# Down projection of a mixture of experts with the weights stationary and 512 tokens moving

## The reference

```
x = x + tanh(g_xattn) * attention(layernorm(x), ctx, ...)
x = x + tanh(g_ffn) * ffn(layernorm(x))
# ffn:
g = einsum('btd,edf->ebtf', x, gate_w)
u = einsum('btd,edf->ebtf', x, up_w)
h = silu(g) * u
expert_out = einsum('ebtf,efd->ebtd', h, down_w)
out = einsum('ebtd,bte->btd', expert_out, combine)
```

## Time and profile before

| | |
|---|---|
| median of 3 runs | 266.81 us (266.63 to 267.21) |
| profiled execution, its own time | 266.45 us |
| its span, first to last instruction | 264.6 us |
| TensorE busy | 235.4 us, 89% |
| weight loads busy | 167.3 us, 63% |
| VectorE busy | 181.1 us, 68% |
| ScalarE, GpSimd busy | 91.5 and 93.4 us |
| mean granted TensorE clock | 0.968 of full speed |

### The profile page before, as it was taken

How to read it: one execution, slowest core, us unless ns; L and a number is a source line. 1 busy time by engine, 2 the same in 40 slices (tenths; PEclk the granted TensorE clock), 3 DMA queues, 4 the chain that set the end, 5 groups by cost and what they waited for, 6 DMA issues and landing times.

```text
span 264.6 us, 3797 instructions
## 1 busy us (share of the span) xinstructions
PE 235.4 (89%) x1275; PEld 167.3 (63%) x1275; DVE 181.1 (68%) x388; ACT 91.5 (35%) x171; POOL 93.4 (35%) x105
## 2 busy tenths in 40 slices
PE   0895695999989999999869899799999999999992
PEld 0762351455645555555525688688888888888882
DVE  2659979467696767776874475968857675776564
ACT  1564224355555665563556421010101010101100
POOL 5364590020374053621430010408934653462000
PEclk9999577799999999999999999999999999999999
DMA  7461660001900002020020000002312211000004
GB/s 207 75 216 45 154 144 20 2 0 24 201 17 1 2 1 59 2 59 0 1 63 0 0 4 0 0 2 61 81 41 59 59 23 39 0 0 2 0 0 160
DMA packets 22259, 12.09 MB, mean 46 GB/s; under 512 B 14784, under 2 KB 21472, under 8 KB 22240
## 3 DMA queue, kind: packets, MB, share of 16 engines
q1 hardware_dynamic: 21936, 11.63, 17.8%
q10 hardware_dynamic: 304, 0.22, 0.5%
HBM read 7.91 MB, written 1.05 MB: 34 GB/s over the span
## 4 chain that ended last, share of the span: by engine, by line
PE 73%; DVE 14%; issue 3%; SPq 3%; DMA 3%; ACT 2%; DVEq 0%
PE bank L955 66%; DVE mneg L811 3%; PE bank L1016 2%; DMA mqk_u<-in_mask_SxS_bc 2%; PE bank L1012 2%; DVE xn L671 1%; SPq L365 1%; DVE x_sb L948 1%; DVE w L853 1%; PE bank L1029 1%; DMA q<-q 1%; PE bank L1021 1%; DVE pT L883 1%; DVE q L889 1%; DVE q L680 1%
## 5 line engine op out<-in xcount | busy, mean ns | idle before, releaser
L955 PE MATMUL bank<-xT,cT 128*128 128x512 f32 x288 | 70.2, 392 | 0.0
L955 PEld LDWEIGHTS bank<-xT,cT 128*128 128x128 f32 x288 | 53.7, 188 | 12.0 <-issue 0.8
L811 DVE TENSOR_REDUCE mneg<-bank 128x4 f32<-128x512 f32 x64 | 43.3, 685 | 20.8 <-PE bank L955 20.4
L636 ACT ACTIVATE pT<-bank 128x512 f32<-128x512 f32 x64 | 38.5, 601 | 31.1 <-PE bank L955 30.1
L623 ACT ACTIVATE pT<-bank 128x512 f32<-128x512 f32 x24 | 14.4, 598 | 84.2 <-PE bank L955 84.2
L955 PE MATMUL bank<-q,kz 112*128 112x512 f32 x64 | 39.0, 611 | 0.0
L955 PEld LDWEIGHTS bank<-w_d,q 128*128 128x128 f32 x288 | 37.1, 188 | 2.8 <-issue 1.3
L955 PE MATMUL bank<-w_d,q 128*128 128x256 f32 x288 | 38.0, 281 | 0.8 <-DVE q L889 0.8
L955 PE MATMUL bank<-kz,q 96*128 96x512 f32 x64 | 28.7, 455 | 6.1 <-DVE mneg L811 5.9
L883 DVE TENSOR_TENSOR pT<-pT,bank 128x512 f32<-128x512 f32 x24 | 16.5, 686 | 16.6 <-PE bank L955 16.3
L874 DVE TENSOR_TENSOR pT<-pT,bank 128x512 f32<-128x512 f32 x24 | 16.4, 682 | 16.7 <-PE bank L955 16.7
(11 more groups left out here) (127 smaller groups left out, 302.8 us busy)
## 6 DMA issues: line engine op xcount, KB each, us to landing
padf<-in_L_ffn_down_w SPq DMA_DIRECT2D x12, 128.0 KB, 2.2
c_sb<-in_ctx SPq DMA_DIRECT2D x2, 512.0 KB, 6.4
q<-cT SPq DMA_DIRECT2D x8, 128.0 KB, 2.4
out<-x_sb SPq DMA_DIRECT2D x4, 256.0 KB, 2.4
q<-xn SPq DMA_DIRECT2D x8, 96.0 KB, 2.2
c_sb<-in_L_ffn_gate_w SPq DMA_DIRECT2D x8, 96.0 KB, 2.1
c_sb<-in_L_ffn_up_w SPq DMA_DIRECT2D x8, 96.0 KB, 2.1
x_sb<-in_x SPq DMA_DIRECT2D x2, 256.0 KB, 3.8
```

Of the source, the lines that this page charges most:

```text
L636: nc.scalar.activation(pT[:, i // 4, i % 4, :], bank[2 + s % 2][:], ACT.Exp, scale=SCALE).then_inc(p_done, 1)
L811: nc.vector.tensor_reduce(mneg[:, r, 4 * hf:4 * hf + 4], bank[n % 2][:].rearrange("p (g k) -> p g k", g=4), X, ALU.max, negate=True).then_ ...
L955: return nc.tensor.matmul(dst, a, b, start=start, stop=stop, skip_group_check=True)
```

## The change

The down projection takes w_d as the stationary operand (two chunks k of 128 output channels) and 512 tokens of h as the moving one: 6 matmuls of 512 columns in place of 12 of 256. The result lies in banks 2 to 5 with output channels on partitions, one bank for each half and chunk. It must be transposed back: the bank is copied to `y_sb` (which lies in `xb_sb`, no longer used by then), by ScalarE for three of the four banks and by VectorE for the last; TensorE transposes 128x128 pieces with the identity into `y_bank` (banks 2 and 3 for half 0, banks 6 and 7 for half 1); VectorE adds them to x_sb, 512 columns at a time.

The order of units changes for tiles 9 to 11: all three for half 0 and then all three for half 1. `END0`, the last unit of half 0, is 20. Half 0 goes back within the loop, behind down(21) on TensorE and behind weigh(22) on VectorE; half 1 at the very end.

```diff
-        ORDER = [(t, h) for h in range(NQ) for t in range(WR)] + [(t, h) for t in range(WR, FT) for h in range(NQ)]
+        ORDER = ([(t, h) for h in range(NQ) for t in range(WR)]
+                 + [(t, h) for t in range(WR, FT - WR) for h in range(NQ)]
+                 + [(t, h) for h in range(NQ) for t in range(FT - WR, FT)])
+        END0 = max(n for n, (_, h) in enumerate(ORDER) if h == 0)
...
+        def y_bank(h, pair):
+
+            return bank[(2, 3, 6, 7)[2 * h + pair]]
...
+            def output_chunk(h, k):
+
+                sc.wait_ge(y_done, 2 * ((END0 if h == 0 else len(ORDER) - 1)) + k + 1)
+                nc.scalar.copy(y_sb[:, h, k], bank[2 + DC * h + k][:]).then_inc(ya_ok, 1)
+
             for n in range(len(UP_SLOT), len(ORDER)):
                 silu(n)
+                if n == min(END0 + UL, len(ORDER) - 1):
+                    output_chunk(0, 0)
+                    output_chunk(0, 1)
+            output_chunk(1, 0)
...
+            def add_outputs(h):
+
+                for p in range(2):
+                    ve.wait_ge(yt_done, 2 * h + p + 1)
+                    t = h * TPH + 2 * p
+                    nc.vector.tensor_tensor(x_sb[:, t:t + 2], y_bank(h, p)[:].rearrange("p (t d) -> p t d", t=2),
+                                            x_sb[:, t:t + 2], ALU.add).then_inc(fin_ok, 1)
...
                 if n + UL < len(ORDER):
                     gated(n + UL)
-
-            for y in range(NB // 2):
-                ve.wait_ge(y_done, 2 * (len(ORDER) - NQ + y // 2) + y % 2 + 1)
-                for t in (2 * y, 2 * y + 1):
-                    ins = nc.vector.tensor_tensor(x_sb[:, t], bank[2 + y][:, t % 2 * D:(t % 2 + 1) * D], x_sb[:, t], ALU.add)
-                ins.then_inc(fin_ok, 1)
+                if n == END0 + 1:
+                    add_outputs(0)
+            ve.wait_ge(y_done, 2 * len(ORDER))
+            nc.vector.tensor_copy(y_sb[:, 1, 1], bank[2 + DC + 1][:]).then_inc(yd_ok, 1)
+            add_outputs(1)
...
-                for u in range(TPH):
-                    ins = three(bank[2 + (h * TPH + u) // 2][:, u % 2 * D:(u % 2 + 1) * D],
-                                [lambda c, i=i: (hh, hl)[i][:, n % 2, toks(u)] for i in range(2)],
-                                [lambda c, i=i: w_d[i][:, s] for i in range(2)], 1, first=(t == 0 and u % 2 == 0))
-                    if u % 2:
-                        ins.then_inc(y_done, 1)
+                for k in range(DC):
+                    three(bank[2 + DC * h + k][:], [lambda c, i=i: w_d[i][:, s, k * P:(k + 1) * P] for i in range(2)],
+                          [lambda c, i=i: (hh, hl)[i][:, n % 2] for i in range(2)], 1, first=(t == 0)).then_inc(y_done, 1)
+
+            def outputs_back(h):
+
+                if h:
+                    pe.wait_ge(*emptied(JOBS[-1]))
+                    pe.wait_ge(*emptied(JOBS[-2]))
+                for k in range(DC):
+                    if k == 0:
+                        pe.wait_ge(ya_ok, 2 if h == 0 else 3)
+                    elif h:
+                        pe.wait_ge(yd_ok, 1)
+                    for u in range(TPH):
+                        ins = nc.tensor.transpose(y_bank(h, u // 2)[:, u % 2 * D + k * P:u % 2 * D + (k + 1) * P],
+                                                  y_sb[:, h, k, toks(u)], ident)
+                        if k and u % 2:
+                            ins.then_inc(yt_done, 1)
...
                 down(n)
+                if n == END0 + 1:
+                    outputs_back(0)
+            outputs_back(1)
```

More of the change, by code:

```diff
@@ L175, in build @@
         pick_n = sb("pick_n", [2 * E, FT * P], U8)
+        y_sb = xb_sb[:].rearrange("p b d -> p (b d)").rearrange("p (h c n) -> p h c n", h=NQ, c=DC)
         pick_r = w_t[:, 0:FT * P]
@@ L244, in build @@
         fin_ok = sem("fin_ok")
+        ya_ok = sem("ya_ok")
+        yd_ok = sem("yd_ok")
+        yt_done = sem("yt_done")
         PHASE_A = [("wkv",), ("c", 0, 0), ("c", 0, 1), ("wq",), ("x", 0, 0), ("x", 0, 1), ("bias",), ("kv", 0),
```

## The result

The changed kernel takes 269.14 us (median of 6 runs, 268.33 to 269.90) against 267.01 us before: ratio 1.008, 95% interval 1.0054 to 1.0105. It is slower by 2.1 us. A second comparison on another occasion gave 1.007 (1.0046 to 1.0095).

A forecast was written before the change was run, and what follows sets the result against it. It took TensorE as the bound (89% busy, full in the feed-forward stage), with another order of work at the end. Terms -0.8 + 0.2 + 2.36 = +1.76 us gave 268.5 us, range 267.5 to 269.6.

The forecast's parts named there:

- The new down: Down projection on TensorE: 6 matmuls of 512 columns take 1.37 us in place of 1.41, 0.04 us less a step.
- the sum over the steps: Down projection gain over the 20 downs ahead of down(20): -0.8 us, bounds -0.4 to -1.2.
- The wait at up(20): TensorE waits ahead of up(20) for GpSimd's split of tile 11's gate and up weights: 0.19, say +0.2 us.
- The tail: From down(20) to the end of the span: +14.50 us against +12.14 before, a loss of 2.36 us.
- The late down(23): Down(23) on TensorE starts at +7.37 us after down(20) where it started at +5.93: +1.44 us.
- the way behind it: After down(23): copy, transposes and adds no longer overlap a projection, making the last add another 1.89 us later.
- the 1.44 us: Delay of down(23), laid to four adds of half 0 queued on VectorE ahead of weigh(23).
- The last transfer: Last output transfer at the end: lands after 2.3 us in place of 3.3, -1.0 us; bounds 2.2 and 3.3.
- Rival 1: Last output transfer lands no sooner, still 3.3 us: +1.0 us, 269.5 us in all; chance 0.12.
- Rival 3: Weight loads limit TensorE, so halving down's loads saves 14 us over 20 steps, some 255 us; chance 0.05.

The follow-up runs named there:

- The first two experiments: Changed kernel with half 0's two adds behind weigh(23): 268.33 us, 1.0038; then also CB(23) issued ahead of half 0's transposes: 268.36 us, 1.0023.
- the form alone: Kernel before with only the new down projection, old order and end, no transposing back (output holds transposed blocks): 266.82 us, ratio 0.9979.
- the order alone: Kernel before with only the new order of units, and the waits of its last adds set accordingly: 267.66 us, ratio 1.0008.
- the wide adds with clears: Kernel before with four last adds of 512 columns for eight of 256, plus four tiny VectorE clears as filling: 267.31 us, ratio 1.0005.
- the changed kernel with clears: Changed kernel plus four tiny clears in VectorE's idle time in the middle of the feed-forward stage: 268.65 us, ratio 1.005.
- the wide adds alone: Kernel before with its eight last adds of 256 columns made four of 512: 266.48 us, ratio 0.9968.
- both half-mixed kernels: Changed kernel, CB(23) first, half 0's adds behind weigh(23), half 1 in old down: 266.07 us, 0.9954; with half 1's last adds 512 wide: 266.31 us, 0.9966.
- the kernel with CB(23) first: Changed kernel with half 0's adds behind weigh(23) and CB(23) issued ahead of half 0's transposes on TensorE: 268.36 us, ratio 1.0023.

## Why the prediction was right, and where it was not

**The new down was priced nearly right, the sum over the steps was too large.** For the down 1.37 us were forecast and the rows show 1.40; a regular step is 4.367 us (forecast 4.35). That is 0.026 us won a step and not 0.04. Besides, I multiplied by 20 downs, and only 17 of them lie between the first full up and down(20). The other three lie ahead of that up. Behind the last of them TensorE idles for VectorE (1.62 us in before, 1.63 in after), and a gain of hundredths ahead of that wait cannot be told from the scatter of the start. 17 x 0.026 is 0.44 us where I had 0.8. Of these 0.44 the waits for GpSimd take 0.18 at up(20) and 0.08 at up(8), and another 0.03 is lost between the first up and down(3), which leaves the 0.15 us measured. The wait at up(8) I had not looked for: its step takes 4.49 us in before (182.07 to 186.56), 0.10 over a regular one, and 4.55 in after, 0.18 over.

**The wait at up(20) was right** in place, releaser and size (0.19 forecast, 0.18 measured, gone when GpSimd's queue is reordered). It does not look as forecast: there is no gap ahead of the first matmul. GpSimd is done at 236.58, just ahead of the 236.62 at which that matmul is due (0.23 us behind CB(18)), and what is lost is the head start of the weight load.

**The tail was right in sign and sequence, and too dear in sum:** 2.36 forecast, 1.92 measured. The late down(23) was forecast at +1.44 and is +1.17; the way behind it +1.89 and is +1.69. The pieces were a little shorter than their rows: the eight transposes hold TensorE for 0.79 us (255.67 to 256.46) in place of 0.96, and weigh(23) starts 1.20 us after the first of the two adds (256.53 to 257.73) in place of 1.39.

**One attribution fell.** I wrote that the 1.44 us are four adds that now stand on the path of the last h. The first two experiments divide them: moving the adds gives back 0.74 us and CB(23) ahead of the transposes another 0.55. I had CB(23) at +3.94 in my own list, behind the transposes, and did not ask who waits for it; weigh(23) does. With the adds ahead of it this waiting is hidden, so the time came out right, but a fix by the forecast's words, moving the adds alone, gives 0.74 us and not 1.44.

**The last transfer was right in size for a wrong reason.** The step "two of the four are now gone" was given -1.0 us, and -0.94 was measured. The landing of the last output itself went from 3.3 to 2.3 us. Of that the crowd is 0.2 us (2.5 against 2.3) and the instruction transfer 0.8. The forecast knew nothing of the instruction transfer, so that the size came out right is luck. The earlier trace rows show 3.3 us; what they were owed to could be read only in the queue of the instruction transfers, which I did not open. Rival 1, in which the 3.3 us stay, is what a changed kernel with an instruction transfer beside its last output would have shown; none of the runs was one.

**Rival 3** (weight loads) is refuted by the form alone. The Trainium skill ("Perfetto Trace Analysis", section Identifying the Most-Contended Engine) names the busy share of weight loads, beside the share of peak arithmetic, as the measure of how near TensorE is to its limit. It does not say what a load fewer is worth, and here it was no guide to that: 144 loads of 188 ns went, and 0.3 us came back in the trace, about 0.6 in the times. Nor did their share stay with the engine's limit: in the windows from 200 to 210 us it falls from 8.92 of 10 us in before to 8.13 in after, where TensorE is busy for all 10.00 us in both. The distance between matmuls was the measure.

```profile
200.00:210.00 10.00, 10.00 (x45) 8.13 (x45) 7.04 (x10) 1.20 (x2) 5.40 (x5) 1.00 0.26 57
```

**The median** is 269.14 and the forecast was 268.5. Of the 2.1 us by which the spans differ, 1.77 lie behind the first full up (1.92 lost in the tail less 0.15 won in the steps), where 1.76 was forecast. That this agrees so closely is luck: a gain 0.45 too large stands against a tail 0.44 too dear. The remaining 0.33 us are the start.

## What to carry to other kernels

Price a wider matmul by the distance of starts in the same stage, not by the count of instructions or weight loads: two of 256 columns cost here what one of 512 does, to 3%. Work that goes back early for the sake of the end must not be queued ahead of what the last units wait for, on any engine: here adds on VectorE and transposes ahead of one small matmul on TensorE cost 1.3 us. When the last transfer takes longer than its fellows, open all queues for that window before blaming the crowd.

## What the runs showed of the hardware that I had not expected

A transfer of instructions (0.01 MB, one packet) that falls beside an output of 256 KB makes that output land 0.8 to 1.0 us later (3.3 us against 2.3 in a pair; 3.3 or 3.4 against 2.5 among four). Whether it falls there hung on four instructions in VectorE's program: 0.9968 without them, 1.0005 with them. When exactly such a transfer is called for stays open; it came among the last outputs, between 262.6 and 264.0 us, in the kernel before, the form alone, the order alone and the wide adds with clears, at 258 us in the changed kernel with clears, and behind the end in the wide adds alone and both half-mixed kernels.

The granted clock near the start also differs between profiles. The same window, 20 to 70 us, of the kernel before and of the kernel with CB(23) first (length, busy time of the five engines, clock, DMA share, GB/s):

```profile
20.00:70.00 50.00, 41.34 (x177) 21.94 (x177) 38.07 (x75) 21.96 (x40) 15.40 (x12) 0.83 0.29 67
```

```profile
20.00:70.00 50.00, 42.86 (x167) 21.85 (x167) 37.33 (x72) 21.45 (x39) 15.22 (x12) 0.76 0.26 60
```

In seven profiles with 0.83 the first full up starts between 171.65 and 172.52 us, in three with 0.76 between 172.68 and 173.19; four with 0.80 have it between 171.59 and 172.93, so the clock is not all of it. No kernel has other work than another in that window, so a difference of one microsecond between two profiles of this family says nothing before both are counted from the same place in the program.
